# Softmax of an attention block: one exponential per head with its sum, in place of one exponential per eight heads

## The chip, the cores and the metric

One core of a Trainium2 chip runs the whole program in one launch. The metric is the device time of that launch in microseconds (us), the median of several runs. Instructions run on five engines: TensorE (PE, with its weight loads shown apart as PEld), VectorE (DVE), ScalarE (ACT), GpSimd (POOL) and SyncE (SP), which here only issues transfers.

## The reference

The input x is 64 sequences of 64 tokens with 512 channels. In float32:

```python
w = weights[subjects]; b = bias[subjects]           # a 64x64 matrix and 64 biases for each sequence
h = einsum('bct,bcd->bdt', x, w) + b[:, :, None]
q, k, v = heads of h @ Wq.T, h @ Wk.T, h @ Wv.T      # 16 heads of 32
scores = q k^T / sqrt(32) + alibi (causal, -inf above the diagonal)
attn = softmax(scores, axis=-1)
x = x + (attn @ v) @ Wo.T
g = einsum('bct,bcd->bdt', x, weights2[conditions])
h = relu(quant8(fwht(g)) @ ternary(w_up).T) ** 2
x = x + quant8(fwht(h)) @ ternary(w_down).T          # fwht: normalized Walsh-Hadamard transform
```

## The kernel before

Two sequences make a pair: 128 rows of tokens, one for each partition. There are 32 pairs, c = 0 to 31. The program is a software pipeline that is written out by hand: in step c of 35, every engine works in a fixed order on the attention of pair c, on the output projection, the second conditioning and the first Hadamard transform of pair c-1, on the FFN's first product and second Hadamard transform of pair c-2, and on the last product of pair c-3. The products of q and k for two pairs (a group) are spread as eight jobs over the two steps before they are needed, four in each (`qk(c, 0)` to `qk(c, 3)`). The conditioning of pair c+4 (`next_cond1`) runs in step c too, while there is such a pair. Engines meet through counting semaphores alone, so the order in which each engine's code stands is the order in which it runs.

In a step, TensorE runs: `scores`, `up`, `down`, `o_product`, `hadamard2`, `qk(c, 0)`, `next_cond1`, `cond2`, `v_product`, `qk(c, 1)`, `hadamard1`, `turn_max`, `turn_p(c, 0)`, `qk(c, 2)`, `turn_p(c, 1)`, `spread_scale`, `qk(c, 3)`, `pv`, `turn_q1`. Many of the products are made of three fp32 products (high and low parts), all on line 367.

The softmax of pair c is worked on in two halves of 8 heads, in the tile `s` (128 x 16 heads x 64). VectorE takes scores out of PSUM and adds the position bias (`add_alibi`, L863), takes each row's maximum (`row_max`, L869), subtracts it (`less_max`, L874). ScalarE takes the exponential of 8 heads in one instruction (`exp`, L684). VectorE sums each row (`exp_sum`, L880) and inverts the sum (`exp_recip`, L885); GpSimd multiplies (`normalize`, L1124); TensorE transposes (`turn_p`, L437). `srow` holds maximum, sum and inverse for each head.

Around it, on ScalarE: `relu`, `square`, `square_hi` (L707, L711, L715) for pair c-2, then `exp(c, 0)`, then `copy_odd` (L720), which takes the odd blocks of the second Hadamard product out of PSUM, `copy_next_qk` (L660), `exp(c, 1)`, `copy_g` (L696), which hands the second conditioning's result `gT` to GpSimd, `copy_v` (L671), `copy_hi` (L654), `spread_k` (L678), `copy_pt` (L688) and `scale_y1` (L700). On VectorE: `fly0` (L945) reads what `copy_odd` wrote, and `fly1` and `fly2` (L264, two instructions each) go on from it; `col_max` (L957) hands the result to `turn_max` on TensorE (L514). On GpSimd: `turn_g` is four instructions on `gT` (L264 too), and `hadamard1` on TensorE (L481) waits for the last. `add_bias` (L837) takes the conditioning out of PSUM; in step 0 it stands behind `exp_recip(0, 1)`. Also in the first steps, the FFN's weights are rounded on ScalarE (`w_abs_sum` L724, `w_round` L729) and clipped on VectorE (`clip_low` L851, `clip_high` L857), and the second of the two weights can only be loaded into its staging tile when the first has been clipped; the weight of the output projection is split on VectorE in step 0 (L821, L826).

Of the kernel before, what the change touches and what calls it, by code (L numbers as in the profile page):

```python
# [30 lines left out]
P = 128  # L31
# [16 lines left out]
def adaln_attn_ffn(nc, x, idx1, bias_table, idx2, w1, wqT, wkT, wvT, woT, w2, upT, downT, cst, out):  # L48
    ctx = ExitStack()
    with ctx:  # L50
# [3 lines left out]
        def sem(name):  # L54
            return ctx.enter_context(nc.semaphore(name))
# [127 lines left out]
        d_max = sem("d_max")  # L183
        d_less = sem("d_less")
        d_sum = sem("d_sum")
        d_recip = sem("d_recip")
# [37 lines left out]
        def pair(p):  # L224
            return 0 <= p < NPAIR
# [413 lines left out]
        def _(act):  # L639
# [41 lines left out]
            def exp(c, half):  # L681
                hs = slice(8 * half, 8 * half + 8)
                act.wait_ge(d_less, 2 * c + half + 1)
                act.activation(s[:, c % 2, hs, :], s[:, c % 2, hs, :], ACT.Exp).then_inc(a_exp, 1)  # L684

# [76 lines left out]
            for c in range(N_STEP):  # L762
# [17 lines left out]
                if next_group(c):  # L780
                    copy_next_qk(c, 0)
                if pair(c):
                    exp(c, 1)
                if c == 1:
                    w_abs_sum(1, 1)
                if pair(c - 1):
                    copy_g(c - 1)
                if pair(c):
                    if c == 0:
                        act.wait_ge(s_wlo, 3)  # L790
                    copy_v(c)
# [24 lines left out]
        def _(dve):  # L816
# [41 lines left out]


            def add_alibi(c, half):  # L860
                hs = slice(8 * half, 8 * half + 8)
                dve.wait_ge(s_s, 2 * c + half + 1)
                dve.scalar_tensor_tensor(s[:, c % 2, hs, :].rearrange("p h k -> p (h k)"), bank[half], DH ** -0.5,  # L863
                                         alibi[:, hs, :].rearrange("p h k -> p (h k)"), ALU.mult, ALU.add).then_inc(d_alibi, 1)

            def row_max(c, half):
                hs = slice(8 * half, 8 * half + 8)
                dve.wait_ge(d_alibi, 2 * c + half + 1)
                dve.tensor_reduce(srow[:, 0, hs], s[:, c % 2, hs, :], AX.X, ALU.max).then_inc(d_max, 1)  # L869

            def less_max(c, half):
                hs = slice(8 * half, 8 * half + 8)
                dve.wait_ge(d_max, 2 * c + half + 1)
                dve.tensor_tensor(s[:, c % 2, hs, :], s[:, c % 2, hs, :], srow[:, 0, hs].unsqueeze(2).broadcast_to([P, 8, T]),  # L874
                                  ALU.subtract).then_inc(d_less, 1)

            def exp_sum(c, half):
                hs = slice(8 * half, 8 * half + 8)
                dve.wait_ge(a_exp, 2 * c + half + 1)
                dve.tensor_reduce(srow[:, 1, hs], s[:, c % 2, hs, :], AX.X, ALU.add).then_inc(d_sum, 1)  # L880

            def exp_recip(c, half):
                hs = slice(8 * half, 8 * half + 8)
                dve.wait_ge(d_sum, 2 * c + half + 1)
                dve.reciprocal(srow[:, 2, hs], srow[:, 1, hs]).then_inc(d_recip, 1)  # L885
# [136 lines left out]
            for c in range(N_STEP):  # L1022
# [6 lines left out]
                if pair(c):  # L1029
                    add_alibi(c, 0)  # L1030
                    add_alibi(c, 1)
                    row_max(c, 0)
                    row_max(c, 1)
                    less_max(c, 0)
                    less_max(c, 1)
                if c == 2:
# [5 lines left out]
                if pair(c - 2):  # L1042
                    square_lo(c - 2, 1)
                if pair(c):
                    exp_sum(c, 0)
                if pair(c - 1):
# [15 lines left out]
                if pair(c + AHEAD) and c > 0:  # L1062
                    dve.wait_ge(p_hlo, c + 3)
                    add_bias(c + AHEAD)
                if pair(c):
                    exp_sum(c, 1)
                if pair(c - 2):
# [134 lines left out]
```

## Time and profile before

| | |
|---|---|
| median of 3 runs | 762.7 us (761.15 to 765.21) |
| the profiled execution: its time | 763.7 us |
| the profiled execution: its span | 761.9 us |
| mean granted TensorE clock | 0.982 of full speed |
| busy: PE, PEld | 727.9 us (96%), 616.3 us (81%) |
| busy: DVE | 668.4 us (88%) |
| busy: ACT | 421.9 us (55%), 844 instructions |
| busy: POOL | 214.3 us (28%) |

The span runs from the first to the last instruction of the profiled execution; the 1.8 us that its time has beyond that lie around it. An engine's busy time counts its instructions from start to end, a waiting one not included unless it waits for a port. Two instructions in a row on one engine can overlap by some hundredths of a microsecond, so the distance from start to start (the pitch below) is what a chain pays.

### The profile page before, as it was taken

What the parts mean: (1) busy time and instruction counts of PE and PEld (TensorE: products, weight loads), DVE (VectorE), ACT (ScalarE), POOL (GpSimd) and SP (SyncE); (2) the same over time, 40 slices, a digit from 0 to 9 for tenths busy, and PEclk for the clock granted to TensorE, in tenths of its full rate; (3) what the DMA queues carried; (4) which work ended last, traced back from release to release, by engine and by line L of the source; (5) the groups of instructions that cost most, each with busy time, mean ns of one, the idle gap of its engine ahead of it and who ended that gap; (6) DMA issues with size and microseconds to landing.
All of it is one profiled execution on the core that took longest, in us unless ns stands there. A gap on an engine that the chain in (4) does not pass through costs nothing.

```text
span 761.9 us, 23166 instructions
## 1 busy us (share of the span) xinstructions
PE 727.9 (96%) x9637; PEld 616.3 (81%) x9671; DVE 668.4 (88%) x1346; ACT 421.9 (55%) x844; POOL 214.3 (28%) x228
## 2 busy tenths in 40 slices
PE   7888999999999999999999999999999999997777
PEld 4777888888888888888888888888888888886643
DVE  3596999999999999999999999999999999988866
ACT  2478566556565565556565565565665665564421
POOL 1123333222333333222333332223333332122300
PEclk9899999999999999999999999999999999998979
DMA  7651111011111111111111110111111010110000
GB/s 235 226 182 37 37 50 41 28 34 52 49 51 50 51 49 27 40 36 51 50 50 51 51 45 23 35 49 50 50 51 50 31 31 31 30 31 16 6 11 28
DMA packets 37422, 39.91 MB, mean 52 GB/s; under 512 B 21189, under 2 KB 21317, under 8 KB 37317
## 3 DMA queue, kind: packets, MB, share of 16 engines
q1 hardware_dynamic: 34180, 32.04, 13.7%
q10 hardware_dynamic: 3136, 6.39, 2.4%
q8 instruction: 76, 1.25, 0.7%
q14 instruction: 30, 0.24, 0.1%
HBM read 30.02 MB, written 8.39 MB: 50 GB/s over the span
## 4 chain that ended last, share of the span: by engine, by line
PE 83%; DVE 8%; ACT 3%; POOL 2%; DMA 2%; issue 1%; SPq 1%; ACTq 0%; DVEq 0%
PE bank L367 43%; PE bank L499 8%; PE bank L535 7%; PE bank L391 4%; PE bank L357 4%; PE bank L481 4%; PE bank L508 4%; PE bank L437 4%; PE bank L454 3%; POOL gT L264 2%; DMA v_kd<-in_L_attn_Wv_dram 2%; PE bank L489 1%; DVE hid L264 1%; PE bank L519 1%; DVE hid L982 1%
## 5 line engine op out<-in xcount | busy, mean ns | idle before, releaser
L264 POOL TENSOR_TENSOR gT<-gT 128x256 f32<-128x256 f32 x124 | 107.2, 884 | 454.7 <-ACT gT L696 452.3
L264 DVE TENSOR_TENSOR hid<-hid 128x512 f32<-128x512 f32 x128 | 100.7, 828 | 0.0
L671 ACT ACTIVATE v_kd<-bank 64x256 f32<-64x256 f32 x128 | 48.5, 379 | 73.6 <-PE bank L367 72.5
L367 PE MATMUL bank<-h_hi,wk_hi 128*128 128x256 f32 x252 | 74.5, 296 | 5.6 <-ACT kT L660 5.6
L367 PE MATMUL bank<-h_hi,wq_hi 128*128 128x256 f32 x256 | 75.0, 293 | 0.0
L367 PE MATMUL bank<-h_lo,wq_hi 128*128 128x256 f32 x256 | 72.6, 284 | 0.0
L367 PE MATMUL bank<-h_hi,wq_lo 128*128 128x256 f32 x256 | 72.6, 283 | 0.0
L367 PE MATMUL bank<-h_hi,wk_lo 128*128 128x256 f32 x252 | 72.0, 286 | 0.0
L367 PE MATMUL bank<-h_lo,wk_hi 128*128 128x256 f32 x252 | 71.9, 285 | 0.0
L707 ACT ACTIVATE late<-bank 128x512 f32<-128x512 f32 x64 | 37.6, 588 | 60.3 <-PE bank L499 60.2
L1124 POOL TENSOR_TENSOR s<-s,srow 128x512 f32<-128x512 f32 x64 | 66.6, 1044 | 11.2 <-DVE srow L885 11.2
L499 PE MATMUL bank<-q1T,up_w 128*128 128x128 bf16 x1024 | 64.5, 222 | 1.3 <-DVE q1T L929 1.3
L499 PEld LDWEIGHTS bank<-q1T,up_w 128*128 128x128 bf16 x1024 | 58.9, 99 | 7.2 <-issue 5.0
L957 DVE TENSOR_REDUCE hid_max<-hid 128x128 f32<-128x1024 f32 x32 | 63.3, 1977 | 0.1
L982 DVE TENSOR_TENSOR hid<-hid,bank 128x1024 f32<-128x1024 f32 x32 | 39.1, 1221 | 25.0 <-PE bank L519 25.0
L720 ACT ACTIVATE hid_odd<-bank 128x256 f32<-128x256 f32 x64 | 24.6, 384 | 63.2 <-PE bank L508 60.8
L367 PE MATMUL bank<-wo_hi,oT_hi 128*128 128x512 f32 x128 | 56.2, 439 | 1.0 <-DVE wo_lo L826 1.0
L535 PE MATMUL bank<-down_w,q2T 128*128 128x512 bf16 x225 | 53.8, 379 | 2.0 <-DVE q2T L990 0.3
L367 PEld LDWEIGHTS bank<-h_hi,wk_hi 128*128 128x128 f32 x252 | 48.4, 192 | 7.6 <-ACT kT L660 6.2
L367 PE MATMUL bank<-wv_hi,h_hi 128*128 128x512 f32 x128 | 54.0, 422 | 0.0
L945 DVE TENSOR_TENSOR hid<-bank,hid_odd 128x256 f32<-128x256 f32 x128 | 45.4, 417 | 6.3 <-ACT hid_odd L720 6.3
L367 PE MATMUL bank<-wv_lo,h_hi 128*128 128x512 f32 x128 | 50.8, 397 | 0.0
(126 smaller groups left out, 1946.9 us busy)
## 6 DMA issues: line engine op xcount, KB each, us to landing
x_in<-in_x_dram SPq DMA_DIRECT2D x32, 256.0 KB, 2.6
x_res<-in_x_dram SPq DMA_DIRECT2D x32, 256.0 KB, 3.4
out_dram<-late SPq DMA_DIRECT2D x32, 256.0 KB, 3.4
w_in<-in_L_cond_weights_dram SPq DMA_DIRECT2D x126, 16.0 KB, 2.4
bias_in<-in_fside_8xS_dram SPq DMA_DIRECT2D x62, 32.0 KB, 3.2
k_bd<-in_L_attn_Wk_dram ACTq DMA_DIRECT2D x1, 1024.0 KB, 5.4
s<-in_L_attn_Wq_dram ACTq DMA_DIRECT2D x1, 1024.0 KB, 6.7
v_kd<-in_L_attn_Wv_dram ACTq DMA_DIRECT2D x1, 1024.0 KB, 11.9
```

Of the source, the lines that this page charges most:

```text
L264: eng.tensor_tensor(dv[:, :, n], sv[:, :, 0], sv[:, :, 1], op).then_inc(done, 1)
L357: mm = pe.matmul(dst[f * T:f * T + T, e, m, :], tokens[r, n:n + T], w[r, :], start=True, stop=True)
L367: mm = pe.matmul(dst, lhs(a, k), rhs(b, k), start=(k == 0 and n == 0), stop=(k == KC - 1 and n == 2))
L391: mm = pe.matmul(dst[:, m // 2, m % 2], qT[rows, (c // 2) % 2, m, t0:t0 + T], k_bd[rows, c % 2, m, :, e * T:e * T + T], start=True, stop=True)
L499: mm = pe.matmul(ps45[:, m * P:(m + 1) * P], up_w[:, k, m * P:(m + 1) * P], q1T[:, k, :], start=(k == 0), stop=(k == KC - 1))
L535: mm = pe.matmul(ring(f + 3, DOWN), q2T[:, k, :], down_w[:, k, :], start=(k == 0), stop=(k == FC - 1))
L671: ins = act.activation(v_kd[b * T:b * T + T, c % 4, e], blocks[e * T:e * T + T, :, b, :], ACT.Copy)
L707: act.activation(half_of(sq, half), bank[4 + half], ACT.Relu).then_inc(a_relu, 1)
L945: dve.tensor_tensor(dst[:, :, n], even, hid_odd[:, 2 * half:2 * half + 2, :], op).then_inc(d_fly, 1)
L957: dve.tensor_reduce(hid_max[:, :], hid[:, 0].rearrange("p m t -> p t m"), AX.X, ALU.max, apply_absolute_value=True).then_inc(d_colmax, 1)
L982: dve.tensor_tensor(hid[:, 1], hid[:, 0], ps_scale.unsqueeze(1).broadcast_to([P, FC, P]), ALU.mult).then_inc(d_scaled, 1)
L1124: pool.tensor_tensor(s[:, c % 2, hs, :], s[:, c % 2, hs, :], srow[:, 2, hs].unsqueeze(2).broadcast_to([P, 8, T]), ALU.mult).then_inc(p_pn, 1)
```

## The change

ScalarE now takes the exponential head by head: 8 instructions of 128x64 in place of one of 128x512. To make the maximum usable as a bias, `add_alibi` computes the negated score, `row_max` takes the minimum of it (which is the negated maximum), and the exponential runs with scale -1 and that minimum as its bias. Each of these instructions also writes its row's sum (`accum_out`). `less_max` and `exp_sum` are gone from VectorE with their semaphores, and `exp_recip` waits for the exponentials. On ScalarE the second half, `exp(c, 1)`, now stands behind `copy_g(c - 1)`, and in step 1 behind `w_abs_sum(1, 1)` as well.

```diff
             def exp(c, half):
-                hs = slice(8 * half, 8 * half + 8)
-                act.wait_ge(d_less, 2 * c + half + 1)
-                act.activation(s[:, c % 2, hs, :], s[:, c % 2, hs, :], ACT.Exp).then_inc(a_exp, 1)
+                act.wait_ge(d_max, 2 * c + half + 1)
+                for j in range(8 * half, 8 * half + 8):
+                    ins = act.activation(s[:, c % 2, j, :], s[:, c % 2, j, :], ACT.Exp, bias=srow[:, 0, j:j + 1], scale=-1.0,
+                                         accum_out=srow[:, 1, j:j + 1])
+                ins.then_inc(a_exp, 1)
...
-                if pair(c):
-                    exp(c, 1)
                 if c == 1:
                     w_abs_sum(1, 1)
                 if pair(c - 1):
                     copy_g(c - 1)
+                if pair(c):
+                    exp(c, 1)
...
-                dve.scalar_tensor_tensor(s[:, c % 2, hs, :].rearrange("p h k -> p (h k)"), bank[half], DH ** -0.5,
-                                         alibi[:, hs, :].rearrange("p h k -> p (h k)"), ALU.mult, ALU.add).then_inc(d_alibi, 1)
+                dve.scalar_tensor_tensor(s[:, c % 2, hs, :].rearrange("p h k -> p (h k)"), bank[half], -DH ** -0.5,
+                                         alibi[:, hs, :].rearrange("p h k -> p (h k)"), ALU.mult, ALU.subtract).then_inc(d_alibi, 1)
...
-                dve.tensor_reduce(srow[:, 0, hs], s[:, c % 2, hs, :], AX.X, ALU.max).then_inc(d_max, 1)
-
-            def less_max(c, half):
-                hs = slice(8 * half, 8 * half + 8)
-                dve.wait_ge(d_max, 2 * c + half + 1)
-                dve.tensor_tensor(s[:, c % 2, hs, :], s[:, c % 2, hs, :], srow[:, 0, hs].unsqueeze(2).broadcast_to([P, 8, T]),
-                                  ALU.subtract).then_inc(d_less, 1)
-
-            def exp_sum(c, half):
+                dve.tensor_reduce(srow[:, 0, hs], s[:, c % 2, hs, :], AX.X, ALU.min).then_inc(d_max, 1)
+
+            def exp_recip(c, half):
                 hs = slice(8 * half, 8 * half + 8)
                 dve.wait_ge(a_exp, 2 * c + half + 1)
-                dve.tensor_reduce(srow[:, 1, hs], s[:, c % 2, hs, :], AX.X, ALU.add).then_inc(d_sum, 1)
-
-            def exp_recip(c, half):
-                hs = slice(8 * half, 8 * half + 8)
-                dve.wait_ge(d_sum, 2 * c + half + 1)
                 dve.reciprocal(srow[:, 2, hs], srow[:, 1, hs]).then_inc(d_recip, 1)
```

ScalarE's queue in the middle of a full step, before (an even or odd step alike but for `kT` or `qT`; `s_up`, `s_f2`, `s_qk`, `s_g`, `s_v` are TensorE's semaphores, `d_less` and `d_max` VectorE's):

```order
L711 ACTIVATE late<-late 128x512 [waits a_relu]
L715 ACTIVATE sq_hi<-late 128x512 [waits a_sq]
L684 ACTIVATE s<-s 128x512 [waits d_less]
L720 ACTIVATE hid_odd<-bank 128x256 [waits s_f2] x2
L660 ACTIVATE kT<-bank 128x256 [waits s_qk]
L684 ACTIVATE s<-s 128x512 [waits d_less]
L696 ACTIVATE gT<-bank 128x2x4x64 [waits s_g]
L671 ACTIVATE v_kd<-bank 64x256 [waits s_v]
```

The same place in the queue now:

```order
L711 ACTIVATE late<-late 128x512 [waits a_relu]
L715 ACTIVATE sq_hi<-late 128x512 [waits a_sq]
L682 ACTIVATE s,srow<-s,srow 128x64 [waits d_max]
L682 ACTIVATE s,srow<-s,srow 128x64 x7
L720 ACTIVATE hid_odd<-bank 128x256 [waits s_f2] x2
L658 ACTIVATE kT<-bank 128x256 [waits s_qk]
L696 ACTIVATE gT<-bank 128x2x4x64 [waits s_g]
L682 ACTIVATE s,srow<-s,srow 128x64 [waits d_max]
L682 ACTIVATE s,srow<-s,srow 128x64 x7
L669 ACTIVATE v_kd<-bank 64x256 [waits s_v]
```

Eight instructions of exponentials stand ahead of `copy_odd`, and eight between `copy_g` and `copy_v`, where one stood ahead of each of `copy_odd` and `copy_g`.

VectorE's queue in step 0, from the scores of pair 0 to the first clipped weight, before:

```order
L869 TENSOR_REDUCE srow<-s 128x8 [waits d_alibi] x2
L874 TENSOR_TENSOR s<-s,srow 128x512 [waits d_max] x2
L880 TENSOR_REDUCE srow<-s 128x8 [waits a_exp]
L885 RECIPROCAL srow<-srow 128x8 [waits d_sum]
L880 TENSOR_REDUCE srow<-s 128x8 [waits a_exp]
L885 RECIPROCAL srow<-srow 128x8 [waits d_sum]
L837 TENSOR_TENSOR h_sum<-bank,bias_in 128x2x4x64 [waits s_h,p_hlo]
L851 TENSOR_SCALAR up_w<-late 128x2048 [waits a_fround]
```

The same place in the queue now:

```order
L870 TENSOR_REDUCE srow<-s 128x8 [waits d_alibi] x2
L875 RECIPROCAL srow<-srow 128x8 [waits a_exp] x2
L837 TENSOR_TENSOR h_sum<-bank,bias_in 128x2x4x64 [waits s_h,p_hlo]
L851 TENSOR_SCALAR up_w<-late 128x2048 [waits a_fround]
L851 TENSOR_SCALAR up_w<-hid 128x2048 [waits a_fround]
```

`add_bias` and the clipping of the weights still stand behind the inverse of the second half's sums, and so behind all 16 heads' exponentials.

## Rows read from the trace of the kernel before

**Rows 1.** 90 to 640 us: busy PE, PEld, DVE, ACT, POOL; clock; DMA share, GB/s
```profile
90.00:640.00 550.00, 548.42 (x7618) 476.13 (x7643) 509.52 (x1046) 321.26 (x661) 166.49 (x175) 1.00 0.14 43
```

**Rows 2.** Timeline of ScalarE in one full step: start, duration, engine, line
```profile
377.95 0.62 ACT L684 ACTIVATE s<-s 128x512 f32<-128x512 f32 x1
380.47 0.85 ACT L720 ACTIVATE hid_odd<-bank 128x256 f32<-128x256 f32 x2 [1.90 <-PE bank L508]
...
383.49 0.60 ACT L696 ACTIVATE gT<-bank 128x512 f32<-128x512 f32 x1 [0.22 <-PE bank L357]
386.46 1.55 ACT L671 ACTIVATE v_kd<-bank 64x256 f32<-64x256 f32 x4 [2.37 <-PE bank L367]
...
391.37 0.61 ACT L688 ACTIVATE pT<-bank 128x512 f32<-128x512 f32 x1
```

**Rows 3.** Timeline of VectorE in the same step
```profile
382.34 1.29 DVE L264 TENSOR_TENSOR hid<-hid 128x512 f32<-128x512 f32 x2
...
383.67 1.83 DVE L264 TENSOR_TENSOR hid<-hid 128x512 f32<-128x512 f32 x2
...
386.03 0.67 DVE L880 TENSOR_REDUCE srow<-s 128x8 f32<-128x512 f32 x1
386.62 1.99 DVE L957 TENSOR_REDUCE hid_max<-hid 128x128 f32<-128x1024 f32 x1
```

**Rows 4.** Timelines of GpSimd (two steps), weight load and TensorE
```profile
384.17 3.44 POOL L264 TENSOR_TENSOR gT<-gT 128x256 f32<-128x256 f32 x4 [14.64 <-ACT gT L696]
...
405.72 3.45 POOL L264 TENSOR_TENSOR gT<-gT 128x256 f32<-128x256 f32 x4 [14.63 <-ACT gT L696]
...
387.67 0.97 PEld L481 LDWEIGHTS bank<-cst_sb,gT 128*128 128x128 f32 x8
...
387.70 1.12 PE L481 MATMUL bank<-cst_sb,gT 128*128 128x128 f32 x8
388.67 0.33 PE L514 MATMUL bank<-cst_sb,hid_max 128*128 128x128 f32 x1
...
392.89 0.86 PE L454 MATMUL bank<-pT,v_kd 64*32 64x64 f32 x64
```

**Rows 5.** GpSimd's L264 from 384.9 to 385.9 us: shortest, median, longest in ns
```profile
L264 POOL TENSOR_TENSOR gT<-gT x2: 786/988/1189, 384.2 to 384.9; 128x256 f32<-128x256 f32 x2
```

**Rows 6.** Timeline of GpSimd in step 31
```profile
706.48 4.64 POOL L264 TENSOR_TENSOR gT<-gT 128x256 f32<-128x256 f32 x4 [14.71 <-ACT gT L696]
```

**Rows 7.** Timeline of ScalarE in step 1: an instruction with accumulator, then the next
```profile
56.90 1.90 ACT L724 ACTIVATE down_w<-hid 128x2048 bf16<-128x2048 f32 x1
58.70 0.19 ACT L724 ACTIVATION_READ_ACCUMULATOR down_w<-hid 128x1 f32 x1
58.79 0.58 ACT L696 ACTIVATE gT<-bank 128x512 f32<-128x512 f32 x1
```

**Rows 8.** Timeline of ScalarE in steps 0 and 1
```profile
39.34 1.99 ACT L729 ACTIVATE hid<-hid,wsum 128x2048 f32<-128x2048 f32 x1
41.23 0.61 ACT L684 ACTIVATE s<-s 128x512 f32<-128x512 f32 x1
...
42.01 0.62 ACT L684 ACTIVATE s<-s 128x512 f32<-128x512 f32 x1
...
52.96 1.91 ACT L724 ACTIVATE down_w<-late 128x2048 bf16<-128x2048 f32 x1 [3.37 <-DMA late<-in_L_ffn_w_down_dram]
```

**Rows 9.** Timeline of VectorE in steps 0 and 2
```profile
43.50 0.65 DVE L837 TENSOR_TENSOR h_sum<-bank,bias_in 128x512 f32<-128x512 f32 x1
...
75.28 1.22 DVE L851 TENSOR_SCALAR down_w<-hid 128x2048 bf16<-128x2048 f32 x1
```

**Rows 10.** Timeline of TensorE in steps 1 and 2
```profile
68.95 0.58 PE L454 MATMUL bank<-pT,v_kd 64*32 64x64 f32 x36 [1.40 <-ACT pT L688]
...
77.25 0.47 PE L508 MATMUL bank<-sq_hi,had_r 128*128 128x512 f32 x1 [1.20 <-DVE sq_lo L936]
...
86.59 0.32 PE L514 MATMUL bank<-cst_sb,hid_max 128*128 128x128 f32 x1
```

More of the change, by code:

```diff
@@ L183, in adaln_attn_ffn @@
         d_max = sem("d_max")
-        d_less = sem("d_less")
-        d_sum = sem("d_sum")
         d_recip = sem("d_recip")
@@ L1033, in _ @@
                     row_max(c, 1)
-                    less_max(c, 0)
-                    less_max(c, 1)
                 if c == 2:
@@ L1043, in _ @@
                     square_lo(c - 2, 1)
-                if pair(c):
-                    exp_sum(c, 0)
                 if pair(c - 1):
@@ L1064, in _ @@
                     add_bias(c + AHEAD)
-                if pair(c):
-                    exp_sum(c, 1)
                 if pair(c - 2):
```

## The prediction

> **What bounds the kernel now.** I first read the busy time by stretch. From 90 to 640 us TensorE is busy for 548.42 of 550 us at full granted clock [rows 1]: the full steps are one unbroken row of matmuls, 21.55 us long each (`turn_g` begins at 384.17 and at 405.72 [rows 4]), and nothing that VectorE or ScalarE are relieved of can shorten them. The change can only matter in two ways: it can open a gap in that row, or it can move the first steps and the last ones, where TensorE waits. So I read the timelines of one full step for what has slack and how much, then those of the first steps.
>
> **What a head's exponential costs.** The trace has none of this shape, so I build it. An instruction of 128x2048 with an accumulator starts at 56.90 and its READ_ACCUMULATOR at 58.70: pitch 1.80 us. The instruction behind the READ starts 0.09 us later although the READ lasts 0.19 us [rows 7]. An exponential of 128x512 has a pitch of 0.52 (its 0.62 less the 0.10 by which that first pair overlaps) [rows 2, 7]. The two give (1.80 - 0.52)/1536 = 0.83 ns an element and 0.147 us for 64 elements. An operand with one value per partition costs 0.09 us more: the pitch of L729 at 2048 elements is 41.23 - 39.34 = 1.89 us against 1.80 [rows 7, 8]. One head: 0.147 + 0.09 + 0.09 = 0.33 us; a half of 8 heads 2.66 us, where it was 0.52. From below: if the per-partition bias is hidden, 0.24 a head. From above: if neither instruction overlaps, 0.246 + 0.09 + 0.19 = 0.53. I take 0.33, because all three parts are pitches that were seen.
>
> The Trainium skill ("ScalarE: Activation LUTs", Rules for kernel authors) budgets about 0.3 us plus 0.83 ns per element for an instruction with such a bias, that is an estimate of 0.35 us a head before any READ, which it does not price. By that budget, with a READ at its seen pitch, the sum would be nearer to the dear case below; the trace so far speaks for the overlap.
>
> **A full step, first half.** `exp(c, 0)` starts at 377.95 and `copy_odd` at 380.47, after an idle 1.90 us [rows 2]. Eight heads end at 377.95 + 2.66 = 380.61: `copy_odd` starts 0.14 us late. That passes through `fly0` and `fly1` to `fly2`; nothing on VectorE makes it up, since `less_max` and the first `exp_sum` end before a wait anyway. Now the tight place. `turn_g` on GpSimd (384.17, 3.44 us) ends at 387.61, the weight load of `hadamard1` starts at 387.67, its first matmul at 387.70 [rows 4]: 0.03 us of slack. And `turn_g` and `fly2` are in each other's way: `fly2` takes 1.83 us where the like `fly1` ahead of it takes 1.29 [rows 3], and one of GpSimd's four takes 1189 ns and another 786 [rows 5]. The times fit turns taken whole: GpSimd's first waits for the end of `fly2`'s first, which waits no more; `fly2`'s second waits for GpSimd's first, and GpSimd's second for that. So if `fly2` is 0.14 us late, GpSimd is 0.14 us late with it, and TensorE stands for 0.14 - 0.03 = 0.11 us. This holds in the 25 steps from c = 3 to c = 27: **+2.8 us**. With the cover gone each further 0.01 us a head costs 0.08 us a step, 2 us in all.
>
> The Trainium skill ("SBUF — State Buffer", on the shared port pair) says that such a pair of instructions takes an exclusive lock and does not share bandwidth. By shared bandwidth the delay would be spread over both and the 2.8 us would be about half; the trace agrees with the lock.
>
> `col_max` ends at 388.61 and `turn_max` starts at 388.67 [rows 3, 4]: as tight, but the second `exp_sum` ahead of it (0.59 us of pitch) is gone, against 0.14 more twice: no cost. It costs again when the first half ends about 0.3 us later than I say.
>
> **A full step, second half.** `copy_g` keeps its place in time: it starts when TensorE has finished (idle 0.22 [rows 2]), and ScalarE is free by 381.6 plus one copy. `exp(c, 1)` now runs from 384.0 to 386.7, and `copy_v`, due at 386.46, starts 0.25 us late. Behind it ScalarE works without a pause until `copy_pt(c, 1)` ends at 391.98; who waits for that is `pv`, at 392.89 [rows 2, 4]. The slack is 0.9 us, so 0.25 costs nothing; it would be used up at 0.41 us a head. The normalization of the second half waits for these exponentials too, but the matmul that needs it is 2 us behind. Nothing.
>
> **The first steps.** Here ScalarE and VectorE are the path. Step 0: the exponentials start at 41.23; the second starts at 42.01, so the copy between them takes 0.26 [rows 8]. Now they end at 41.23 + 16 x 0.333 + 0.26 = 46.8, and with the result's landing and the inverse `add_bias(4)` starts at about 47.1 where it started at 43.50 [rows 9]: +3.6. Behind it on VectorE stand 8 us of clipping and splitting of weights and then the scores of pair 1; the second FFN weight is loaded when the first clip is done, so `w_abs_sum`, which waited 3.37 us for that load at 52.96 [rows 8], starts 3.6 later as well, at about 56.5. In step 1 ScalarE is then full: the two halves are 2 x (2.66 - 0.52) = 4.3 us longer, and of that some 0.7 us go into an idle time ahead of the first and some 2.1 into the one ahead of `copy_v` (in a full step 2.37 [rows 2]): 3.6 + 4.3 - 2.8 = 5.1. So `pv(1)`, which waited for ScalarE at 68.95 [rows 10], comes at about 73.9: +5.0. In step 2 VectorE drops `less_max` (two pitches, 1.2 us) ahead of the last clip (75.28 [rows 9]) and the low parts, for which `hadamard2` waited at 77.25 [rows 10]: +3.8. But the eight heads ahead of `copy_odd` start at about 80.7 and end at 83.4, 1.6 us after it could run, so `fly1` and `fly2` now lie wholly beside `turn_g`. That is the state of step 31, where `turn_g` takes 4.64 us [rows 6]; VectorE's chain, made longer by it, ends with `col_max`, and `turn_max(0)` moves from 86.59 [rows 10] to about 92.0. **+5.4 us** for the first steps, between 4 and 6.5 by what the load and the turns do.
>
> **The last steps.** In steps 28 to 31 `copy_g` no longer stands behind `exp(c, 1)` and starts 0.2 us earlier. GpSimd may then get the first turn, `hadamard1` gains 0.2 and VectorE, a turn behind, loses up to 0.5, with `exp_sum` gone. From -0.7 to +0.9; I take +0.2.
>
> **Sum.** 2.8 + 5.4 + 0.2 = 8.4 us on the profiled execution's 763.7 us, that is 1.1%; on the median of 762.7 us it gives 771.
>
> **The rivals.**
> - *As forecast*, 0.31 to 0.38 us a head: 767 to 781 us. Chance 0.62. At 0.38 the delay is 0.52, TensorE stands 0.49 us in 25 steps (12 us), and the first steps cost about 6.5.
> - *Cheap heads*, up to 0.30: no gap in the full steps. At 0.24 the first half ends at 379.9, well before 380.47. The first steps cost 16 x 0.09 = 1.5 us less in step 0, 1.5 less in step 1, and the pile-up of step 2 is nearly gone: about +1. 763 to 767 us. For it: ScalarE has 1.90 us idle before `copy_odd`. Against: the price of a per-partition operand is seen in the trace. Chance 0.20.
> - *Dear heads*, 0.40 or more, because short instructions and READs do not overlap. At 0.53 the half takes 4.24 us, `copy_odd` is 1.7 late, `turn_g` is wholly beside VectorE (4.64 for 3.44: 1.1 us of waiting), and `col_max` ends about 1.9 us after its time: 1.9 x 25 = 48, with the first steps some 57: 820 us. Already at 0.40, 785. Chance 0.14.
> - *Faster*: one mechanism, VectorE's relief in the first steps. If ScalarE's late exponentials did not carry into step 2, the `less_max` of steps 1 and 2 (1.2 us each) would be won: about 760 us. It decides where 16 heads cost less than the 2.27 us from 41.23 to 43.50 less the copy, that is at 0.11 us a head, and 64 elements alone take 0.147. Chance 0.04.
>
> **Numbers.** About 0.5% (3.8 us) is what a measurement of this kernel can tell from no change. The likeliest is 771 us. The range 763.5 to 781 us leaves out the dear heads and the faster case, 0.18. Faster 0.04; within 0.5% the cheap heads but for the 0.02 of them above 766.5 us, 0.18; slower the rest, 0.78.
>
> **What the profile after would show.** Right: L682 in pairs with a READ, pitch together 0.33; `copy_odd` without idle time ahead of it; a wait of TensorE on GpSimd's L264 of about 0.1 us in each full step; steps near 21.65 us; ScalarE above 570 us busy; the first clip of `up_w` near 47.7. Wrong, and with it the sum: a pitch that is not 0.33, `add_bias(4)` before 46.5, a full step that still takes 21.55 us, or a new wait at `pv` or at the second transposes.

## The result, and the profile after

The changed kernel takes **772.07 us** (median of 4 runs, 771.67 to 772.95), beside 763.96 us for the kernel before on the same chip: ratio 1.0109 [1.0082, 1.0135]. It is slower by 1.1%, about what was forecast (771). The profiled execution took 771.67 us, with a span of 769.9 us at a mean granted clock of 0.978; before it was 763.7, 761.9 and 0.982. Three executions of the runs below (886 us in `e1`, 2828 us in `e10`, 1286 us in the kernel before beside `e5`) were far slower than the others of their kernel, and no ratio counts them.

The busy times and the costliest new groups, from the page of the kernel after:

```profile
PE 734.2 (95%) x9671; PEld 616.6 (80%) x9671; DVE 598.1 (78%) x1218; ACT 550.8 (72%) x1804; POOL 217.1 (28%) x228
L682 ACT ACTIVATE s<-s,srow 128x64 f32<-128x64 f32 x512 | 170.2, 334 | 1.2 <-DVE srow L870 1.2
L682 ACT ACTIVATION_READ_ACCUMULATOR s<-s,srow 128x1 f32 x512 | 96.4, 188 | 0.0
```

VectorE has lost 70 us of work and ScalarE has gained 129. Neither moves the end by itself: between 90 and 640 us TensorE is as busy as it was [rows 1], at full clock.

```profile
90.00:640.00 550.00, 548.40 (x7600) 472.93 (x7602) 449.74 (x945) 422.25 (x1413) 173.09 (x180) 1.00 0.14 44
```

The same full step as in [rows 2] to [rows 4], 7.62 us later in the program's time. First ScalarE's timeline, then VectorE's, GpSimd's and TensorE's:

```profile
385.57 0.34 ACT L682 ACTIVATE s<-s,srow 128x64 f32<-128x64 f32 x1
385.90 0.34 ACT L682 ACTIVATE s<-s,srow 128x64 f32<-128x64 f32 x1
...
388.22 0.71 ACT L720 ACTIVATE hid_odd<-bank 128x256 f32<-128x256 f32 x2
...
391.11 0.60 ACT L696 ACTIVATE gT<-bank 128x512 f32<-128x512 f32 x1 [0.74 <-PE bank L355]
...
388.62 1.42 DVE L935 TENSOR_TENSOR hid<-bank,hid_odd 128x256 f32<-128x256 f32 x4 [0.30 <-ACT hid_odd L720]
...
391.40 1.83 DVE L262 TENSOR_TENSOR hid<-hid 128x512 f32<-128x512 f32 x2
...
391.79 3.56 POOL L262 TENSOR_TENSOR gT<-gT 128x256 f32<-128x256 f32 x4 [14.81 <-ACT gT L696]
...
395.40 1.16 PE L479 MATMUL bank<-cst_sb,gT 128*128 128x128 f32 x8
```

The eight heads take 388.22 - 385.57 = 2.65 us, 0.333 us each as forecast. `copy_odd` follows them at once, where it stood idle for 1.90 us in [rows 2]. `fly2` begins 0.39 us ahead of `turn_g` (before: 0.50 [rows 3, 4]), `turn_g` lasts 3.56 us where it lasted 3.44, and the matmuls of `hadamard1` begin as soon as it ends. The third `turn_g` begins at 110.53 and the one 24 steps on at 629.86, so a step is (629.86 - 110.53)/24 = 21.639 us; before, from 103.91 to 621.30, it was 21.558. The profile lists no wait of TensorE there: between the start of the last matmul ahead of `hadamard1` and that of its first one lie 0.19 us, where 0.11 lay before, and since the ends of matmuls are modelled, its busy time hides the difference.

The first steps, in timelines of ScalarE, VectorE, TensorE and GpSimd, for [rows 8 to 10]:

```profile
42.01 0.33 ACT L682 ACTIVATE s<-s,srow 128x64 f32<-128x64 f32 x1
...
53.56 0.60 ACT L692 ACTIVATE oT_hi<-bank 128x512 fp32r<-128x512 f32 x1 [0.40 <-PE bank L452]
...
47.83 0.65 DVE L837 TENSOR_TENSOR h_sum<-bank,bias_in 128x512 f32<-128x512 f32 x1
...
74.01 1.05 PE L452 MATMUL bank<-pT,v_kd 64*32 64x64 f32 x64 [1.85 <-ACT pT L688]
...
93.19 0.33 PE L512 MATMUL bank<-cst_sb,hid_max 128*128 128x128 f32 x1 [0.72 <-DVE hid_max L947]
...
86.97 4.29 POOL L262 TENSOR_TENSOR gT<-gT 128x256 f32<-128x256 f32 x4 [14.77 <-ACT gT L696]
```

The first exponential already begins 0.78 us later than in [rows 8]. So does the rounding of a weight just ahead of it on ScalarE (40.12 for 39.34), and in the fourteen traces of this document the first exponential begins anywhere from 39.53 to 42.79. So each start here is read less 0.78. Then `add_bias(4)` is 3.55 us late, `pv(1)` 4.28 and `turn_max(0)` 5.82.

Where the 8.0 us of the two profiled executions lie:

| part | before | after | difference |
|---|---|---|---|
| to the first exponential | 41.23 | 42.01 | +0.78 |
| first exponential to third `turn_g` | 62.68 | 68.52 | +5.84 |
| 24 full steps to the 27th `turn_g` | 517.39 | 519.33 | +1.94 |
| 27th `turn_g` to the end | 140.6 | 140.0 | -0.6 |

The same four parts are read in every run below. "First steps" is the second row, "a step" the third row divided by 24, "last steps" the fourth.

### The profile page after: what moved, and what is told of

Its sections match the earlier page's. It is cut to its first block, busy times and chain, and to the rows that moved or that the text cites. A ratio compares the mean times of both kernels' runs of the same rounds, so it can differ in the third digit from the quotient of the medians.

```text
span 769.9 us, 24032 instructions
## 1 busy us (share of the span) xinstructions
PE 734.2 (95%) x9671; PEld 616.6 (80%) x9671; DVE 598.1 (78%) x1218; ACT 550.8 (72%) x1804; POOL 217.1 (28%) x228
## 4 chain that ended last, share of the span: by engine, by line
PE 81%; DVE 8%; ACT 6%; DMA 2%; POOL 1%; issue 1%; SPq 1%; ACTq 0%; DVEq 0%
PE bank L365 41%; PE bank L497 8%; PE bank L533 7%; PE bank L389 4%; PE bank L479 4%; PE bank L355 4%; PE bank L435 4%; PE bank L506 3%; PE bank L452 3%; ACT s L682 2%; DVE hid L262 2%; DMA v_kd<-in_L_attn_Wv_dram 2%; PE bank L487 1%; DVE hid_max L947 1%; PE bank L517 1%; POOL gT L262 1%
## 5 line engine op out<-in xcount | busy, mean ns | idle before, releaser
L262 POOL TENSOR_TENSOR gT<-gT 128x256 f32<-128x256 f32 x124 | 109.7, 905 | 457.9 <-ACT gT L696 455.4
L682 ACT ACTIVATE s<-s,srow 128x64 f32<-128x64 f32 x512 | 170.2, 334 | 1.2 <-DVE srow L870 1.2
L262 DVE TENSOR_TENSOR hid<-hid 128x512 f32<-128x512 f32 x128 | 103.6, 850 | 0.0
L682 ACT ACTIVATION_READ_ACCUMULATOR s<-s,srow 128x1 f32 x512 | 96.4, 188 | 0.0
L926 DVE TENSOR_TENSOR sq_lo<-late,sq_hi 128x512 fp32r<-128x512 f32 x64 | 44.0, 687 | 24.3 <-ACT sq_hi L715 24.1
L533 PE MATMUL bank<-down_w,q2T 128*128 128x512 bf16 x256 | 60.5, 379 | 0.3 <-DVE q2T L980 0.3
```

Source lines behind the costliest of these rows:

```text
L262: eng.tensor_tensor(dv[:, :, n], sv[:, :, 0], sv[:, :, 1], op).then_inc(done, 1)
L533: mm = pe.matmul(ring(f + 3, DOWN), q2T[:, k, :], down_w[:, k, :], start=(k == 0), stop=(k == FC - 1))
L682: ins = act.activation(s[:, c % 2, j, :], s[:, c % 2, j, :], ACT.Exp, bias=srow[:, 0, j:j + 1], scale=-1.0, accum_out=srow[:, 1, j:j + 1])
L926: dve.tensor_tensor(sq_lo[:, ms, :], sq[:, ms, :], sq_hi[:, ms, :].bitcast(F32), ALU.subtract).then_inc(d_sqlo, 1)
```

## The experiments

Twelve kernels ran, in three groups. The groups ran on different chips; the kernel before, run beside each, had medians of 761.56, 764.11 and 762.44 us, and each ratio is to those runs.

### Which place costs what: old form in the first steps, and only there new

In `e1` the old `exp`, `less_max` and `exp_sum` are used in steps 0 to 2, in `e2` from step 3 on:

```diff
+        def whole(c):            # the old form of a pair's softmax
+            return c < 3         # e2: c >= 3
```

> Steps 0 to 2 as in the kernel before (one exponential for 8 heads, subtraction and sums on VectorE, second half ahead of copy_g), all later steps as changed. My theory: about 5.8 us of the loss are lost on the path of the first steps and 1.9 in the full steps. Then the fourth turn_g on GpSimd starts as early as in the kernel before (within 0.5 us, but for the opening transfers), the full steps stay at 21.64 us, and the time is about 1.5 us above the kernel before, ratio 1.002. Rival, the loss is spread over the run by the 960 more instructions of ScalarE: 29 of 32 pairs still have them, so 7 us remain, ratio 1.009.

> The reverse: steps 0 to 2 as changed, all later steps as in the kernel before. My theory: the full steps are at 21.56 us, the first steps keep their loss of about 5.8 us, and nothing is won in the last steps: ratio 1.0075. Rival, the loss of the first steps is made up later if the full steps have their old form (VectorE or GpSimd catch up): ratio below 1.003. Rival, spread loss: 3 of 32 pairs have it, ratio 1.001.

`e1`: 768.85 us, ratio 1.0084 [1.0062, 1.0105]. `e2`: 767.44 us, 1.0071 [1.0047, 1.0095]. In the traces the two places separate cleanly. `e1` has the first steps of before (62.71 us) and the long full step, 21.643 us with a `turn_g` of 3.57; `e2` has the first steps of after (68.47 us) and the step of before, 21.563. So the two costs are independent of each other. But `e1`'s time missed its number: its full steps explain 24 x 0.085 = 2.0 us, and by the ratio 6.4 were measured. What the rest is comes out below, under the clock.

### What makes the full step longer

`e3` lets `copy_odd` run between the seventh and the eighth head from step 3 on; `e4` puts one more exponential ahead of the eight, so that `copy_odd` is 0.33 us later still.

```diff
...
-                    exp(c, 0)
+                    exp(c, 0, range(7) if c >= 3 else range(8))
                 if pair(c - 2):
                     copy_odd(c - 2, 0)
                     copy_odd(c - 2, 1)
+                if pair(c) and c >= 3:
+                    exp(c, 0, range(7, 8))
```

```diff
+                if half == 0 and c >= 3:       # e4
+                    act.activation(spare[:, :], s[:, c % 2, 0, :], ACT.Exp, bias=srow[:, 0, 0:1], scale=-1.0,
+                                   accum_out=spare_sum[:, :])
```

> As changed, but from step 3 on the eighth head of the first half is computed behind copy_odd instead of ahead of it. The same work and the same number of instructions. My theory (copy_odd 0.13 us late makes fly2 late, and that makes GpSimd late by the lock): copy_odd is on time with about 0.2 us idle ahead of it, GpSimd's four instructions take 3.44 us again and not 3.56, and a full step takes 21.56 us: 1.9 us less than the changed kernel, about 770 us where the changed kernel has 772. Rival, the load itself (more instructions and accumulator reads on ScalarE) costs the 0.08 us a step: the step stays at 21.64 us.

> As changed, but from step 3 on one more instruction of the same kind (head 0 again, into a tile that nobody reads) runs ahead of the first half: 0.33 us more ahead of copy_odd, and nothing else. By the lock theory GpSimd is late by the same 0.33 us and TensorE by all of it: turn_g about 3.89 us, a full step 21.97 us, 8 us more in all (780 us). If the two engines shared bandwidth instead, about half of it: 21.80 us, 4 us more. If the step's end hung on ScalarE's whole load with slack left, nothing.

`e3`: 770.31 us, 1.011 [1.0083, 1.0137], a step of 21.533 us. `e4`: 780.89 us, 1.0249 [1.0222, 1.0275], a step of 21.960 us. Timelines of VectorE and GpSimd in a full step, first of `e3`, then of `e4`:

```profile
387.84 1.83 DVE L262 TENSOR_TENSOR hid<-hid 128x512 f32<-128x512 f32 x2
388.33 3.45 POOL L262 TENSOR_TENSOR gT<-gT 128x256 f32<-128x256 f32 x4 [14.80 <-ACT gT L697]
```

```profile
393.56 1.83 DVE L264 TENSOR_TENSOR hid<-hid 128x512 f32<-128x512 f32 x2
393.60 3.89 POOL L264 TENSOR_TENSOR gT<-gT 128x256 f32<-128x256 f32 x4 [14.81 <-ACT gT L701]
```

`turn_g` ends 3.93 to 3.95 us after `fly2` has begun: 0.49 + 3.45 in `e3`, 0.04 + 3.89 in `e4`, 0.39 + 3.56 in the kernel after, 0.50 + 3.44 before [rows 3, 4]. So the delay of `copy_odd` reaches TensorE whole, less the slack: the extra head of 0.33 us makes `turn_g` 3.89 - 3.56 = 0.33 us longer, and a step 0.32.

That alone does not tell turns from an even sharing, since two engines that share could also be done with both works at a fixed time. What tells them apart is `fly2` itself: it takes 1.83 us whether `turn_g` joins it 0.49 us after its start (`e3`) or 0.04 us (`e4`), and only GpSimd's first instruction stretches, from 0.79 to 1.24 us. The engine that is second waits for the whole instruction of the first. The Trainium skill ("SBUF — State Buffer", Who interferes with whom) says that two such instructions take an exclusive lock and the second fully blocks, and the trace agrees.

### What the accumulator costs, and what it saves

`e5` leaves the accumulator out and sums on VectorE as before; the exponentials stay head by head with the bias.

```diff
...
-                                         accum_out=srow[:, 1, j:j + 1])
+            def exp_sum(c, half):
+                hs = slice(8 * half, 8 * half + 8)
+                dve.wait_ge(a_exp, 2 * c + half + 1)
+                dve.tensor_reduce(srow[:, 1, hs], s[:, c % 2, hs, :], AX.X, ALU.add).then_inc(d_sum, 1)
...
```

> As changed (head by head, bias from srow, second half behind copy_g), but without the accumulator: the sums are taken by exp_sum on VectorE as before. This prices the accumulator reads. My theory: a head costs 0.24 us in place of 0.333, the first half 1.92, so copy_odd is on time and a full step takes 21.56 us; the first steps lose 16 x 0.24 instead of 16 x 0.333 us in step 0 and in step 1, some 2.5 to 3 us less than the 5.8 of the change, less what the two sums cost there. Ratio 1.004. Rival, the loss of the full steps comes from something else than the length of the first half (the earlier sums, the moved second half): the step stays at 21.64 us.

`e5`: 773.07 us, 1.0132 [1.0096, 1.0167]. The time was a miss, and it is the most useful of the twelve. The timeline of the full step:

```profile
385.42 2.00 ACT L683 ACTIVATE s<-s,srow 128x64 f32<-128x64 f32 x8
...
387.46 0.69 DVE L875 TENSOR_REDUCE srow<-s 128x8 f32<-128x512 f32 x1 [1.15 <-ACT s L683]
387.94 0.84 ACT L720 ACTIVATE hid_odd<-bank 128x256 f32<-128x256 f32 x2 [0.52 <-PE bank L507]
388.06 0.68 DVE L891 TENSOR_TENSOR x<-bank,x_res 128x512 f32<-128x512 f32 x1
388.66 1.41 DVE L940 TENSOR_TENSOR hid<-bank,hid_odd 128x256 f32<-128x256 f32 x4
...
391.44 1.84 DVE L263 TENSOR_TENSOR hid<-hid 128x512 f32<-128x512 f32 x2
...
391.64 3.75 POOL L263 TENSOR_TENSOR gT<-gT 128x256 f32<-128x256 f32 x4 [14.62 <-ACT gT L696]
```

The price was right: 8 heads take 2.00 us, from start to start 0.24 each, and `copy_odd` is on time again, with 0.52 us idle ahead of it. But now VectorE is late. `exp_sum` waits 1.15 us for the exponentials, which end at 387.4, and stands ahead of `add_x` and `fly0` on VectorE. `fly0` has no wait at all here, so what it follows is its own queue, no longer `copy_odd`. `fly2` begins 0.20 us ahead of `turn_g`, and 0.20 + 3.75 is 3.95 again. A step is 21.838 us, that is 6.7 us more in 24 steps; the first steps take 66.53 us, 3.85 more than before. The exponentials are shorter than in the kernel after, and the kernel loses more in each step: the accumulator's 0.09 us a head buys the 0.59 us of `exp_sum` out of the queue ahead of `fly0`. This is read from `e5`'s trace; no further run moved `exp_sum` in the queue by itself.

The Trainium skill ("ScalarE: Activation LUTs", What ACT_TABLE_LOAD costs) gives 186 ns plus 0.833 ns an element, 93 more for a per-partition operand and 93 less by overlap; that is an estimate of 0.239 us for a head without accumulator, and `e5` agrees. The budget of the same page's Rules that the prediction weighed (0.35 us) leaves the overlap out; the measured 0.24 decides.

### What the move is worth

`e6` moves `exp(c, 1)` behind `copy_g` in the kernel before and changes nothing else; `e12` is the changed kernel with the move undone.

```diff
+                if pair(c):                    # e12; e6 is the reverse, on the kernel before
+                    exp(c, 1)
                 if c == 1:
                     w_abs_sum(1, 1)
                 if pair(c - 1):
                     copy_g(c - 1)
-                if pair(c):
-                    exp(c, 1)
```

> The kernel before with only the order changed: exp(c, 1), one instruction, behind copy_g(c - 1). My theory: no effect in the full steps (copy_g waits for TensorE anyway, copy_v is due later), 21.56 us. In steps 28 to 31 copy_g comes 0.2 us earlier; there the changed kernel won 0.5 us. If the move is what won it, this kernel wins it too; if it was VectorE's relief (no exp_sum ahead of col_max), it wins nothing. Ratio 0.999 to 1.000.

> The changed kernel with exp(c, 1) ahead of copy_g again, as in the kernel before, now eight heads long. Theory: copy_g, which is ready when TensorE ends (391.1 in the changed kernel, ScalarE idle 0.74 before it), comes after eight heads at 2.66 us, so 2.5 us late; turn_g starts 2.5 us late, at 394.3, fly2 is then free of it (1.3 us, not 1.83) and turn_g lies beside col_max only; hadamard1 waits 2 to 2.4 us in each full step: a step of 23.6 to 24.0 us, time 820 to 830 us, ratio 1.075 to 1.09. Rival: turn_g beside col_max is free of turns (2.94 us) and hadamard1 waits only 1.6 us: 812 us. If the move buys nothing: 772 us.

`e6`: 764.84 us, 1.0019 [1.0002, 1.0036], first steps 62.70 us and a step of 21.560: alone the move gains nothing. `e12`: 803.85 us, 1.0534 [1.0514, 1.0554]. With eight heads ahead of `copy_g` the move decides, by 32 us, but less than I expected of it. Timelines of `e12`:

```profile
385.42 1.28 DVE L262 TENSOR_TENSOR hid<-hid 128x512 f32<-128x512 f32 x2
387.60 2.92 POOL L262 TENSOR_TENSOR gT<-gT 128x256 f32<-128x256 f32 x4 [16.60 <-ACT gT L696]
390.58 1.16 PE L479 MATMUL bank<-cst_sb,gT 128*128 128x128 f32 x8 [1.08 <-POOL gT L262]
387.23 2.03 DVE L947 TENSOR_REDUCE hid_max<-hid 128x128 f32<-128x1024 f32 x1
```

`hadamard1` waits 1.08 us, and a step is (660.94 - 114.25)/24 = 22.779 us. My 2 to 2.4 us had two errors. The eight heads begin in the 0.74 us that ScalarE stands idle ahead of `copy_g`, so `copy_g` is 1.9 us late, not 2.5. And a later `turn_g` meets no `fly2`: it takes 2.92 us instead of 3.56, although `col_max` runs beside it. 1.9 - 0.64 is 1.3 us, and a step is 1.14 us longer than in the kernel after.

### Which route is the first steps' path

`e7` clips the FFN's weights and splits the weight of the output projection ahead of the first `exp_recip`, so that in step 0 VectorE works while ScalarE takes the exponentials.

```diff
...
+                if c == 0:
+                    clip_low(0, 0)
+                    dve.wait_ge(p_hlo, c + 3)
+                    add_bias(c + AHEAD)
+                    clip_low(0, 1)
+                    exp_recip(0, 0)
+                    hi_part("wo")
+                    exp_recip(0, 1)
+                    lo_part("wo", d_whi, 4)
...
```

> As changed, but VectorE in step 0 no longer waits for the exponentials before the other work: clip, add_bias(4), clip, inverse of the first half, high parts of wo, inverse of the second half, low parts. If the loss of the first steps comes through add_bias(4) and the weights standing behind the second inverse, as I said, split_o(0) moves up by about 1.9 us (then ScalarE's copy_o bounds it, which the exponentials themselves make late) and so does all that follows: ratio 1.0085. If all of the 5.8 us came through VectorE's queue, 4 us would come back (1.0055). If the path is ScalarE's alone from the start, nothing.

`e7`: 770.68 us, 1.0105 [1.0069, 1.0141]; first steps 67.43 us, a step of 21.635. The timelines of VectorE, TensorE and ScalarE, and last TensorE's clock (columns as in [rows 1]):

```profile
45.19 0.20 DVE L875 RECIPROCAL srow<-srow 128x8 f32<-128x8 f32 x1 [0.17 <-ACT s L682]
...
56.53 0.69 DVE L879 TENSOR_TENSOR oT_lo<-bank,oT_hi 128x512 fp32r<-128x512 f32 x1 [3.99 <-ACT oT_hi L692]
...
49.56 0.58 PE L365 MATMUL bank<-h_hi,wk_hi 128*128 128x256 f32 x1 [1.54 <-ACT v_kd L669]
...
55.01 0.86 PE L452 MATMUL bank<-pT,v_kd 64*32 64x64 f32 x64
...
74.56 0.85 PE L452 MATMUL bank<-pT,v_kd 64*32 64x64 f32 x64 [1.84 <-ACT pT L688]
...
55.90 0.60 ACT L692 ACTIVATE oT_hi<-bank 128x512 fp32r<-128x512 f32 x1 [0.41 <-PE bank L452]
...
46.00:54.00 8.00, 6.46 (x35) 6.06 (x35) 5.90 (x6) 7.07 (x24) 4.23 (x3) 0.57 0.61 199
```

The same places in the kernel after:

```profile
49.16 0.39 PE L365 MATMUL bank<-h_hi,wk_hi 128*128 128x256 f32 x1
...
52.67 0.86 PE L452 MATMUL bank<-pT,v_kd 64*32 64x64 f32 x64
...
56.00 0.68 DVE L879 TENSOR_TENSOR oT_lo<-bank,oT_hi 128x512 fp32r<-128x512 f32 x1
```

VectorE's wait of 4.24 us for the exponentials has shrunk to 0.17, and it comes back as one of 3.99 us for `copy_o` (L692), which copies what `pv(0)` gave. `pv(1)` is not a bit earlier: 74.56 - 42.41 = 32.15 us after the first exponential, against 32.00 in the kernel after and 27.72 before. But this does not show that VectorE's queue was not the path, because something else changed in the same trace. `qk(0, 2)` (the row at 49.56) begins 7.15 us after the first exponential in both kernels; then in `e7` TensorE's granted clock is 0.57 from 46 to 54 us, where it was 1.00, and `pv(0)` and with it `copy_o` come 1.94 us later than in the kernel after (13.49 us after the first exponential, for 11.55). That is the 1.9 us by which `split_o` (L879), the next instruction on VectorE, was to move up.

`e3`, which does not touch step 0, shows the other half. Its timelines of ScalarE and VectorE:

```profile
54.35 0.60 ACT L693 ACTIVATE oT_hi<-bank 128x512 fp32r<-128x512 f32 x1 [0.41 <-PE bank L452]
...
55.05 0.68 DVE L882 TENSOR_TENSOR oT_lo<-bank,oT_hi 128x512 fp32r<-128x512 f32 x1
```

Its clock was low at the same place and its `copy_o` 1.71 us late (54.35 - 41.09 = 13.26), and yet `split_o` began 13.96 us after the first exponential, for 13.99 in the kernel after, and `pv(1)` 31.98. So in the kernel after `copy_o` has 1.7 us to spare or more, and `split_o`, which waits there for nothing but the work ahead of it, hangs on VectorE's queue. What `e7`'s order would give at full clock is open; its ratio fits the 1.0085 expected for it and the 1.0109 of the kernel after alike.

### The clock in the first steps

The changed kernel's trace has a stretch in which TensorE ran at a lower clock, just behind `pv(1)`; columns as in [rows 1]:

```profile
74.00:78.00 4.00, 3.99 (x109) 3.30 (x110) 3.29 (x6) 2.63 (x3) 0.00 (x0) 0.57 0.02 4
```

A granted 0.57 is mostly the lower of the two levels, 1.2 GHz instead of 2.4. TensorE had waited 1.36 us for VectorE's `wsum` and 1.85 us for `pT` shortly ahead of it. To see whether those waits bring it about, `e9` fills four of the waits of steps 0 and 1 with spare matmuls that nothing reads.

```diff
...
+                if c == 0:
+                    keep_clock(9, fill, bank[4])
...
+                if c == 1:
+                    keep_clock(7, fill, bank[4])
```

> As changed, with 27 more matmuls in the four waits of TensorE in steps 0 and 1 (before qk(0, 1), before turn_p(0, 0), before w_total(1), before pv(1)), whose results nobody reads. In the changed kernel's trace the granted clock is 0.57 of full speed from 74 to 78 us, right after these waits, and the scores of pair 2 take 1.98 us for 1.10. If the waits cause that stretch, it is gone, the scores take 1.10 us, and the fourth turn_g starts 1 to 2 us earlier (108.5 to 109.5 for 110.5 us): ratio 1.009. If the stretch has another cause, it stays, and the time with it.

`e9`: 772.51 us, 1.0127 [1.0095, 1.0159]. Its clock is at 1.00 from 40 to 100 us and its first steps take 67.28 us instead of 68.52. But `e3`, `e4` and `e7`, with no fills, have 1.00 from 68 to 84 us as well and first steps of 67.26, 67.27 and 67.43, while `pv(1)` comes 32.0 us after the first exponential in the kernel after, `e3` and `e9` alike. (These three had their low stretch earlier, 0.79 from 40 to 56 us; in `e3` and `e4` it made `copy_o` late, and nothing behind it.) So a low clock behind `pv(1)` costs 1.2 us; it also stays away without the fills, and the fills gained nothing that the time shows. That the waits cause it is not shown.

### Both cures at once, and the last steps

`e8` has the old form in steps 0 to 2 and, from step 3, `copy_odd` between the seventh and the eighth head. `e10` is the same with the old form from step 28 on too, so that the new form stands in the full steps alone. `e11` has the new form in steps 28 to 31 alone.

```diff
+            return c < 3                       # e8, with e3's split
+            return c < 3 or c >= 28            # e10, with e3's split
+            return c < 28                      # e11
```

> Old form in steps 0 to 2; new form from step 3, with copy_odd between the seventh and the eighth head. Theory (the cost is made of two places, the first steps and a copy_odd that is late in each full step): both are gone. First exponential to third turn_g 62.7 us (before 62.68), a full step 21.53 us (before 21.56), so 0.7 us less than before in 24 steps, and the last steps as the granted clock there makes them (137.5 to 143.7 us in the runs so far). Ratio to before 0.999 to 1.001. Rival 1, from the run with the old first steps, whose time was 0.3 to 0.5% above what its two places give: the new form costs something in the last steps, or lowers the granted clock there: ratio 1.003 to 1.005 with the full steps still at 21.53. Rival 2: the full steps are not 21.53 when the old form stands ahead of them.

> As the run with both cures, but the old form also from step 28 on: the new form only in steps 3 to 27, where VectorE's relief can buy nothing and ScalarE's load should cost nothing. Theory of two places: ratio 0.999 to 1.001, the same as the other. If the excess of the run with the old first steps lies in the last steps, this kernel is 0.3 to 0.5% below the one with both cures and equal to before. If new exponentials in the full steps cost something that no matmul waits for (a lower clock at the ends), both are at 1.003 to 1.005.

> Old form in steps 0 to 27, new form in steps 28 to 31 alone. Theory: first steps and full steps are those of before (62.7 us, 21.56 us a step); in the last steps VectorE is relieved of less_max and exp_sum where TensorE waits for it, and turn_g takes 4.15 us where it took 4.64: 0.5 us less, ratio 0.999. Rival: the last steps are where the excess of the run with the old first steps comes from: ratio 1.003 to 1.005.

`e8`: 763.73 us, 1.0009 [0.9989, 1.0029], a step of 21.535 us. `e10`: 761.63 us, 0.9986 [0.997, 1.0002], a step of 21.539. `e11`: 762.68 us, 1.0004 [0.9987, 1.0021], a step of 21.560. With both places cured the new form ties with the old one, within 0.3%, though in `e8` VectorE is busy for 410 us between 100 and 600 us instead of 463, and ScalarE for 389 instead of 293. `e10` is lowest, by 0.14%, and its interval reaches 1: no version beats the kernel before by more than can be told.

`e8` differs from `e1` in the place of `copy_odd` alone, and its time is by its interval at most 0.3% above that of the kernel before. What goes with `e1`'s excess is the clock. Windows from 600 to 740 us, columns as in [rows 1], of the kernel after, `e6` and `e7`:

```profile
600.00:740.00 140.00, 130.58 (x1612) 107.02 (x1610) 113.49 (x233) 97.73 (x329) 37.92 (x38) 0.95 0.08 25
```

```profile
600.00:740.00 140.00, 125.14 (x1509) 102.87 (x1514) 121.82 (x252) 69.94 (x140) 36.27 (x37) 0.91 0.07 21
```

```profile
600.00:740.00 140.00, 126.40 (x1609) 103.75 (x1614) 116.14 (x242) 97.62 (x329) 37.93 (x38) 1.00 0.08 25
```

| run | clock, 600 to 740 us | last steps, us |
|---|---|---|
| `e7` | 1.00 | 137.5 |
| `e5` | 0.98 | 139.3 |
| `e2` | 0.97 | 138.4 |
| `e10` | 0.96 | 138.0 |
| after | 0.95 | 140.0 |
| before, `e1`, `e3`, `e4`, `e9` | 0.93 | 140.6, 141.6, 143.3, 143.5, 141.8 |
| `e8`, `e11` | 0.92 | 143.1, 142.9 |
| `e6` | 0.91 | 143.7 |

The last steps took between 137.5 and 143.7 us, longer at a lower clock in the main, with the old form near both ends of the table. In the 29 runs of the kernel before in the last group, time falls with the mean clock in the same way: 763.8 to 766.2 us in the seven at 0.980 or below, 760.1 to 763.1 us in the thirteen at 0.989 or above; a line through all 29 gives 3.4 us for 0.010, and one through the eleven beside `e1` 2.8. The medians of the mean clock were 0.978 for `e1` and 0.987 for the kernel before beside it. That is 2.5 to 3.1 of its 6.4 us; with the 2.0 us of its full steps 1.3 to 1.9 us is left, which five runs don't settle.

Nor is the clock independent of the kernel. In the four runs of `e5` its mean was 0.989 to 0.991 and in those of `e9`, on the same chip, 0.976 to 0.978; in the five of `e1` it was 0.973 to 0.982 and in those of `e3` and `e4` 0.973 to 0.976, where the kernel before had 0.980 to 0.991 beside them. On the chip of the last group `e8` and `e11`, with the new form in the last steps, have a mean of 0.983 over 24 runs, the kernel before and `e10`, with the old form there, 0.986 over 40. Whether the new form lowers the clock at the end, by what would be 1 us, is not shown and not excluded.

## Why the prediction was right

**The head's price.** 0.333 us forecast, 0.333 measured, in steps 0 to 31. The three pitches that it was built from add up as if each were by itself: `e5` took one away and 0.24 was left.

**The full step.** The chain from eight heads by `copy_odd` and `fly2` to `turn_g` was right link by link, and `e3` and `e4` moved its first link in both directions. Its size was a little too large: 0.11 us a step forecast, 0.081 measured. The sign that I gave for it, a wait of TensorE on `turn_g` in the profile, is not there to see: it shows only in the distance between starts. `fly2` is 0.11 us late, not 0.14, against a slack of 0.03. Over 24 steps that is 1.9 us, for 2.8 forecast over 25. The lock was right, but my test of it was not: I said that shared bandwidth would halve the delay, and it is the length of `fly2` that tells the two apart.

**The second half.** `copy_g` kept its place, and no wait of TensorE on `copy_v` or `copy_pt` appeared in the full steps. The step costed at nothing did cost nothing; `e12` shows what it would have cost without the move, 1.14 us a step.

**The first steps.** 5.4 us forecast, 5.84 measured, and the agreement is partly luck. At `pv(1)` I said +5.0, and it was +4.28: the sum left out that VectorE also drops `less_max` ahead of step 1's exponentials (`split_o` is 3.34 us late, the first exponential of pair 1 only 58.51 - 55.58 - 0.78 = 2.15). Then 1.2 us came from the low clock behind `pv(1)`, which I had not reckoned with; without it the first steps cost 4.6 us (67.26 - 62.68 in `e3`). The reason for the +3.6 holds as far as the traces go: `add_bias(4)` moved by 3.55 us, the first clip with it (48.39 less 0.78 is 47.6, for 47.7), and `split_o` stayed on VectorE's queue when `copy_o` was 1.7 us later in `e3`. That moving this work ahead wins it back is not shown; in `e7` the clock took it away. One part was wrong. The reload of the staging tile, which I had put on the path, wasn't on it: `w_abs_sum` began 1.57 us late (55.31 against 52.96, less 0.78), not 3.6, and the exponentials behind it still waited 1.20 us for VectorE's `row_max`. The pile-up of step 2 was right: eight heads from 82.05 to 84.7, `turn_g` at 4.29 us, `turn_max(0)` 5.8 us late.

**The last steps.** +0.2 us forecast within -0.7 and +0.9. The turns did change there: `turn_g` takes 4.15 us in the new form (after, `e1`, `e11`) where it takes 4.64 in the old one [rows 6]. `e6` shows that the move brings this and not VectorE's relief. GpSimd's timeline of `e6` in step 31:

```profile
706.24 4.15 POOL L264 TENSOR_TENSOR gT<-gT 128x256 f32<-128x256 f32 x4 [15.59 <-ACT gT L696]
```

What that does to the time is hidden by a spread of 6 us with the clock; `e11` alone, at 1.0004 [0.9987, 1.0021], leaves room for the forecast and for its opposite.

**A sign that was wrong.** I said that ScalarE would be above 570 us busy; it is 550.8. A busy time counts the overlap of two instructions once, and even the pitches add only 32 x (16 x 0.333 - 2 x 0.52) = 137 us to 421.9. The pitch was the sign to go by.

## What to carry to other kernels

Here, taking 70 us of work off VectorE was worth nothing, since TensorE is the bound; what the change did to the time was decided by what the work on its new engine stands ahead of. Read the queue of the engine that takes the work: here the eighth of eight heads cost 0.08 us a step, and one instruction in another place gave it back. And when the cure of one route changes nothing, look in the same trace for what holds the next instruction up: in `e7` it was a low clock of TensorE, as large as the gain that was hoped for.

## What the runs showed of the hardware

**Two engines in turns.** `fly2` on VectorE and `turn_g` on GpSimd, each with both operands in SBUF, give a constant: `turn_g` ends 3.92 to 3.97 us after `fly2` has begun, in the full steps of all thirteen traces in which they meet, with `fly2` from 0.02 to 0.50 us ahead, and `fly2` itself takes 1.82 to 1.84 us. Free of each other they take 1.28 and 2.92 us (`e12`). `col_max`, a reduction with one operand, overlapped `turn_g` in `e12`, and neither was longer than elsewhere by more than 0.05 us (2.03 and 2.92 us). The Trainium skill ("SBUF — State Buffer", Who interferes with whom) states both, and the trace agrees.

**The accumulator.** It is a second instruction of 188 ns, of which the one behind it hides about 0.09 us; it costs 0.333 - 0.239 = 0.094 us a head, as much at 64 elements as at 2048 [rows 7].

**The clock at the ends.** In the full steps TensorE's granted clock was 1.00 in every run; from 600 to 740 us it lay between 0.91 and 1.00, and one program's time differed by up to 6 us with the mean clock. In step 0 it was 0.57 over 8 us of `e7` and 1.00 in the same place of the kernel after, and the twelve matmuls of 128x256 from 49.56 on took 2.74 us in `e7`, where the kernel after took 1.54. An effect of 0.5% in this kernel is read from the starts of one instruction in two places of the trace (here `turn_g`; kernels of one form agree to about 0.01 us a step), and not from times of one or two runs.
